# Moving row constants, root guess and statistics between VectorE, GpSimd and ScalarE in a graph-attention and mixture-of-experts kernel

## The reference

```
h   = layernorm(x) @ W.T + b_W
e   = leaky_relu((h @ a1)[:, None] + (h @ a2)[None, :] + b_a, slope 0.2)
x   = x + softmax(where(adj > 0, e, -9e15), axis=1) @ h
z   = layernorm(x)
p   = softmax(z @ gate_w + gate_b); keep the two largest of 16, scaled to sum 1
out = x + sum over the two experts k of p_k * ((silu(z @ w1_k) * (z @ w2_k)) @ w3_k)
```

## Time and profile before

| | |
|---|---|
| time of the kernel, median of 3 runs | 1756.96 us (1756.46 to 1762.68) |
| the profiled execution, own time | 1744.11 us |
| span of its profile | 1742.3 us |
| TensorE busy | 1519.6 us (87%) |
| VectorE busy | 1443.1 us (83%) |
| ScalarE busy | 1332.6 us (76%) |
| GpSimd busy | 464.9 us (27%) |

### The profile page before, as it was taken

The page is one execution under the profiler, slowest core; times in us unless marked ns, Lnnn a source line. Parts: engine busy times, 40 slices in busy tenths (PEclk is TensorE's granted clock), DMA queues, the critical chain, the costliest instruction groups (busy, mean ns, idle before and its releaser), DMA issues.

```text
span 1742.3 us, 24866 instructions
## 1 busy us (share of the span) xinstructions
PE 1519.6 (87%) x8110; PEld 840.4 (48%) x8111; DVE 1443.1 (83%) x1946; ACT 1332.6 (76%) x1804; POOL 464.9 (27%) x641
## 2 busy tenths in 40 slices
PE   5678699899989998998999899989999948999991
PEld 5545354455445444544454455445555525666660
DVE  6799999989998999999899989997896753444445
ACT  4989899889888997998799889878786634555550
POOL 6600000210024031403220240114024253555551
PEclk9998999999999999999999999999999978999995
DMA  6888778748865784887488648855432434222227
GB/s 187 299 311 302 238 255 265 234 141 259 262 204 181 255 266 135 260 245 253 133 272 271 207 156 268 255 180 147 135 113 75 139 68 159 74 73 74 74 73 298
DMA packets 127715, 339.40 MB, mean 195 GB/s; under 512 B 16962, under 2 KB 48898, under 8 KB 127490
## 3 DMA queue, kind: packets, MB, share of 16 engines
q1 hardware_dynamic: 106208, 304.06, 54.4%
q0 software_dynamic: 17056, 27.17, 5.9%
q10 hardware_dynamic: 4354, 6.92, 1.2%
HBM read 309.57 MB, written 28.51 MB: 194 GB/s over the span
## 4 chain that ended last, share of the span: by engine, by line
PE 39%; DVE 34%; issue 16%; POOL 4%; ACT 3%; DMA 3%; SPq 0%; ACTq 0%; DVEq 0%; POOLq 0%
PE pair L975 18%; DVE probs L1279 17%; DVE ring L1223 14%; PE pair L1054 8%; PE pair L960 5%; PE pair L1070 4%; ACT ring L713 2%; PE pair L1061 2%; DMA ring<-res_d 1%; PE pair L1050 1%; DVE part L1223 1%; POOL numT L601 1%; POOL numT L604 1%; POOL ln L591 1%; PE pair L987 1%
## 5 line engine op out<-in xcount | busy, mean ns | idle before, releaser
L975 PE MATMUL pair<-probs,X 128*128 128x512 f32 x2048 | 1009.5, 610 | 0.8 <-ACT probs L764 0.7
L764 ACT ACTIVATE probs<-probs,ebias 128x1024 f32<-128x1024 f32 (+1 forms) x576 | 601.2, 1046 | 179.5 <-DVE probs L1279 177.6
L1279 DVE SCALAR_TENSOR_TENSOR probs<-s1row,ns,pair 128x1024 f32<-128x1024 f32 (+1 forms) x576 | 654.5, 1154 | 68.2 <-PE pair L960 66.3
L1223 DVE CUSTOM_DVE_ANT_0 ring<-urow,ring 128x2048 int8<-128x2048 f16 x256 | 586.1, 2291 | 10.2 <-ACT ring L713 10.2
L713 ACT ACTIVATE ring<-stage,neghalf 128x1024 int8<-128x1024 int32 x512 | 575.2, 1141 | 1.5 <-DMA stage<-in_adj 1.2
L960 PEld LDWEIGHTS pair<-diag,ring 128*128 128x128 fp8e5 x4096 | 264.2, 98 | 461.6 <-DVE probs L1279 238.8
L975 PEld LDWEIGHTS pair<-probs,X 128*128 128x128 f32 x2048 | 345.9, 191 | 217.7 <-issue 215.6
L960 PE MATMUL pair<-diag,ring 128*128 128x128 bf16 x4096 | 325.9, 220 | 125.9 <-DVE probs L1279 103.0
L1553 DVE COPY probs<-pair 128x256 f32<-128x256 f32 x144 | 61.1, 425 | 138.6 <-PE pair L1061 126.2
L685 POOL DMA_INDIRECT res_d<-probs x144 | 138.9, 964 | 133.4 <-ACT probs L868 129.7
L1054 PE MATMUL pair<-ring,probs 128*128 x288 | 159.3, 635 | 4.9 <-issue 4.0
(11 more groups left out here) (237 smaller groups left out, 769.3 us busy)
## 6 DMA issues: line engine op xcount, KB each, us to landing
stage<-in_adj SPq DMA_DIRECT2D x512, 512.0 KB, 4.4
probs<-xd_d SPq DMA_DIRECT2D x144, 65.0 KB, 1.9
ring<-res_d SPq DMA_DIRECT2D x16, 512.0 KB, 9.5
ring<-in_L_ffn_w SPq DMA_DIRECT2D x2, 2048.0 KB, 11.7
ring<-xmid_d SPq DMA_DIRECT2D x1, 4096.0 KB, 13.5
out<-ring ACTq DMA_DIRECT2D x8, 512.0 KB, 6.8
s1row<-s_d SPq DMA_DIRECT2D x7, 512.0 KB, 7.2
xres<-in_x POOLq DMA_DIRECT2D x7, 512.0 KB, 12.1
```

The lines of the kernel that those rows point to most:

```text
L764: act.activation(probs[:, n % PR, 0:wide], probs[:, n % PR, 0:wide], ACT.Exp, bias=ebias[:, j:j + 1], scale=RISE).then_inc(probs_ready, 1)
L975: m = pe.matmul(acc[q][:, lo:hi], X[:, j, :], probs[:, n % PR, lo:hi], start=(j == 0), stop=(j == NT - 1))
L1223: dve.tensor_tensor_reduce(m, urow[:, c * CH:(c + 1) * CH], m, CODE, NO_EDGE, ALU.subtract, ALU.max, part[:, k, c:c + 1]).then_inc(piece_d ...
L1279: dve.scalar_tensor_tensor(out=probs[:, n % PR, 0:wide], in0=s1row[:, q, 0:wide], scalar=ns2[:, j:j + 1], in1=Tp[n % 2][:, 0:wide], op0=AL ...
```

## The change

- Row constants: VectorE keeps only the maximum over chunks (`row_max`, at step 58); the rest of `row_end` moves to GpSimd as six operations, with `kS` and `kB` of the other sign. It is called for block 0 and 1 before GpSimd's loop, and for block b+2 between the destinations and the scatter of block b.
- Root guess: `new_root` goes; GpSimd computes the guess in one operation.
- Gate base: `gate_base` goes, with the wait at VectorE's first `logits`. Each block's `gate_logits` multiplies by the standard deviation itself. `sd0` and `nm0` move to tiles of their own, as they now live to the end.
- Signs of block 0: one half per group for `g` = 0 to 4, two from `g` = 5 as before.
- Second layer norm: `new_stats` goes. ScalarE forms each row's sum (`row_sums`, two tiles a step from step 31 in place of VectorE's step 36) and, when GpSimd has given the negative mean, the sum of squared differences (`row_squares`, from step 36). Both write a throw-away result to PSUM and the sum through the accumulator output. `row_sums` waits for the same `xres_in` as `new_stats` did. In host 8 they stand at 26 and 31, and the later steps move by two.
- `last_norm` has two operations and one wait more.

```
-    CHAIN_AT = 59
+    CHAIN_AT = 58
+    DIAG_AT = 61
-            return dict(stats=36, per=2, root=42, top=46, ranks=54, slots=56, weights=61)
-        return dict(stats=26, per=2, root=32, top=38, ranks=46, slots=48, weights=51)
+            return dict(stats=31, per=2, squares=36, top=46, ranks=54, slots=56, weights=61)
+        return dict(stats=26, per=2, squares=31, top=40, ranks=48, slots=50, weights=53)
...
+            def row_end(b):
+                w = slice(0, BLOCKS[b])
+                pool.wait_ge(vmax, b + 1)
+                plink(pool.tensor_scalar(mrow[:, w], rmax[:, w], kS[:, 0:1], kB[:, 0:1], ALU.mult, ALU.add))
+                pool.tensor_scalar(crow[:, w], mrow[:, w], 1.0 / RISE - 1.0, None, ALU.mult)
+                plink(pool.tensor_tensor(hmax[:, w], scol[:, ROW0[b]:ROW0[b + 1], 0], mrow[:, w], ALU.subtract))
+                plink(pool.tensor_scalar(hmax[:, w], hmax[:, w], 0.0, None, ALU.max))
+                plink(pool.tensor_tensor(crow[:, w], crow[:, w], hmax[:, w], ALU.subtract))
+                if b >= 1:
+                    pool.wait_ge(d_ready, b)
+                pool.tensor_scalar(cdiag[:, w], crow[:, w], Cc[:, 0:1], EDGE_ONE, ALU.add, ALU.mult
+                                   ).then_inc(c_ready, 1)
...
+                pool.wait_ge(sum_rows, b + 1)
+                pool.tensor_scalar(r(2), st2[:, 0:n, 0], -1.0 / D, None, ALU.mult).then_inc(nm_ready, 1)
                 pool.wait_ge(st2_ready, b + 1)
...
+                plink(pool.tensor_scalar(r(3), st2[:, 0:n, 1], 1.0 / D, EPS, ALU.mult, ALU.add))
+                plink(pool.tensor_scalar(ln2I[:, 4, 0:n], ln2I[:, 3, 0:n], -0.5, GUESS, ALU.mult, ALU.add))
...
-                pool.tensor_tensor(lg, pgs[:, 0:n, :], cols[:, ROW0[b]:ROW0[b + 1], 2:2 + E], ALU.add)
-                plink(pool.tensor_tensor(t2, per_e(sg[:, :], b), per_t(ln2[:, 2, 0:n], b), ALU.mult))
+                rows = slice(ROW0[b], ROW0[b + 1])
+                pool.tensor_tensor(ln2[:, 0, 0:n], ln2[:, 2, 0:n], nm0[:, rows], ALU.subtract)
+                plink(pool.tensor_tensor(lg, cols[:, rows, 2:2 + E], per_t(sd0[:, rows], b), ALU.mult))
+                pool.tensor_tensor(t2, per_e(sg[:, :], b), per_t(ln2[:, 0, 0:n], b), ALU.mult)
+                plink(pool.tensor_tensor(lg, lg, pgs[:, 0:n, :], ALU.add))
...
-                if 5 <= g < NG:
-                    for i in range(early, early + 2):
+                if g < NG:
+                    for i in range(early, early + (2 if g >= 5 else 1)):
                         sign(0, i)
-                    early += 2
+                    early += 2 if g >= 5 else 1
...
+            def row_sums(b, k):
+                if k == 0:
+                    act.wait_ge(xres_in[b % 2], 16 * (b // 2 + 1))
+                    act.wait_ge(proj_read, ROUND0[b + 1])
+                ins = act.activation(acc[b % 2][:, k * P:(k + 1) * P], xres[:, b % 2, k, 0:D], ACT.Identity,
+                                     accum_out=st2[:, k, 0:1])
+                if k == BLOCKS[b] - 1:
+                    ins.then_inc(sum_rows, 1)
+
+            def row_squares(b, k):
+                if k == 0:
+                    act.wait_ge(nm_ready, b + 1)
+                ins = act.activation(acc[b % 2][:, k * P:(k + 1) * P], xres[:, b % 2, k, 0:D], ACT.Square,
+                                     bias=ln2[:, 2, k:k + 1], scale=1.0, accum_out=st2[:, k, 1:2])
+                if k == BLOCKS[b] - 1:
+                    ins.then_inc(st2_ready, 1)
```

More of the change, by code:

```diff
@@ L667, in scatter_last @@
                             in_=xres[:, LQ, c * LN + k, :], in_offset=None).then_inc(disp[c], 16)
-            gate_base()
+            row_end(0)
+            row_end(1)
             for b in range(LAST):
@@ L676, in _ @@
                 destinations(b, 0)
+                if b + 2 < NB:
+                    row_end(b + 2)
                 for c in range(2):
@@ L828, in _ @@
                     if b >= 1:
-                        k = j - route_units(b)["top"]
-                        if 0 <= k < BLOCKS[b - 1]:
-                            normal_rows(b - 1, k)
+                        units = route_units(b)
+                        for k in range(BLOCKS[b - 1]):
+                            if j == units["stats"] + k // units["per"]:
+                                row_sums(b - 1, k)
+                            if j == units["squares"] + k // units["per"]:
+                                row_squares(b - 1, k)
+                            if j == units["top"] + k:
+                                normal_rows(b - 1, k)
                     if b >= 1 and j == route_units(b)["slots"]:
                         weights(b - 1)
-                    if b + 1 < NB and j == CHAIN_AT + 2:
+                    if b + 1 < NB and j == DIAG_AT:
                         make_diag(b + 1)
@@ L1214, in _ @@
             wlink(dve.tensor_scalar(Cc[:, :], Cc[:, :], 1.0, None, ALU.add))
-            dve.tensor_scalar(kS[:, :], S2, -1.0 / (CODE * U_SPAN), None, ALU.mult)
-            wlink(dve.scalar_tensor_tensor(out=kB[:, :], in0=S2, scalar=-(1.0 - U_MID) / U_SPAN, in1=b2,
-                                           op0=ALU.mult, op1=ALU.add))
+            dve.tensor_scalar(kS[:, :], S2, 1.0 / (CODE * U_SPAN), None, ALU.mult)
+            wlink(dve.scalar_tensor_tensor(out=kB[:, :], in0=S2, scalar=(1.0 - U_MID) / U_SPAN, in1=b2,
+                                           op0=ALU.mult, op1=ALU.subtract))
             def maxima(b, i):
@@ L1224, in maxima, with row_max @@
                                          ALU.subtract, ALU.max, part[:, k, c:c + 1]).then_inc(piece_done, 1)
[L1226 to L1228 removed]
+            def row_max(b):
                 w = slice(0, BLOCKS[b])
[L1230 to L1236, removed]
[L1237 to L1252 removed]
+                dve.wait_ge(piece_done, PIECE0[b + 1])
+                if b >= 1:
+                    dve.wait_ge(c_ready, b)
+                dve.tensor_reduce(rmax[:, w], part[:, w, :], AX.X, ALU.max).then_inc(vmax, 1)
             ready = 0
@@ L1264, in _ @@
                 maxima(0, i)
-            for step in range(5):
-                row_end(0, step)
+            row_max(0)
             def logits(b, j):
@@ L1415, in route @@
             def route(b, j, units):
-                for k in range(BLOCKS[b]):
-                    if j == units["stats"] + k // units["per"]:
-                        new_stats(b, k)
-                if j == units["root"]:
-                    new_root(b)
                 for step in range(TOPS):
@@ L1439, in _ @@
                     if b + 1 < NB and j == CHAIN_AT:
-                        row_end(b + 1, 0)
-                        row_end(b + 1, 1)
-                    if b + 1 < NB and j == CHAIN_AT + 1:
-                        for step in range(2, 5):
-                            row_end(b + 1, step)
+                        row_max(b + 1)
                     if b >= 1:
@@ L1463, in last_norm @@
                 ins.then_inc(st2_ready, 1)
[L1464 removed]
+                rlink(dve.tensor_tensor(lg, cols[:, ROW0[LAST]:NT, 2:2 + E], per_t(sd0[:, ROW0[LAST]:NT], LAST),
+                                        ALU.mult))
+                last_rlink()
+                dve.tensor_tensor(lg, lg, pgs[:, 0:LN, :], ALU.add)
                 dve.wait_ge(st2_ready, LAST + 1)
```

76 lines of the change are left out of this document (14 added, 62 removed).

## The result

The changed kernel takes 1783.78 us (median of 4 runs, 1781.48 to 1787.24), the kernel before 1759.82 us (4 runs, 1756.46 to 1764.73) beside it: 1.0138 times the time, 95% interval 1.0112 to 1.0163. That is 24.0 us slower; forecast were 23, and 1780 us.

What follows compares the result with a forecast made beforehand. VectorE was taken to bound hosts 1 to 6 up to about step 57, TensorE hosts 7 and 8. Terms -4.9 - 1 + 22.5 + 6 + 0.4 = +23.0 us, added to the median of the runs, gave 1780 us, range 1752 to 1803.

Steps and rivals of the forecast that it cites:

- The stall: Step 31, hosts 2 to 6: ScalarE stands at row_sums for the DMA into xres; logits 44 late by 3.6 us.
- S: Time in host 2 when ScalarE goes on after the DMA lands: 459.9 us, bounds 458.0 and 463.2.
- VectorE's relief of 1.9 us: Statistics and root VectorE no longer computes, ahead of logits 44: 1.9 us a host, forecast as lost in the wait.
- The price of a sum: ScalarE's cost for each of 16 new sum and square operations: taken 0.40 us, bounds 0.25 and 0.57.
- Hosts 2 to 6: Stall plus 0.9 us for later gate logits: +4.5 us per host, +22.5 for five, bounds -0.7 and +10.6 each.
- Host 7: TensorE leads; ScalarE stands 5 to 6 us, plus two sums and an exponential (1.8): +6 us, 3 to 9.
- Host 1: Its DMA is issued some 35 us ahead of step 31: no stall, VectorE saves time, -1 us.
- Host 8 and the end: Host 8: no accumulating DMA and TensorE leads, 0; last_norm has two small operations on the path, +0.4 us.
- Prologue: Before host 0: early signs hidden, small operations cheaper, diagonals start at 88.9 against 93.76 us, -4.9 us.
- the slip of the loop: Prologue: maxima starve GpSimd, the 13th group gets its tiles at about 60.7 us, the loop slips by 2.4 us.
- the fast case: Rival at step 31, hosts 2 to 6: stall absorbed, VectorE's relief arrives; -16 us, 1741 us; chance 0.13.
- The slow case: Rival: DMA takes 12 to 14 us, sums cost 0.5 or more; +9 per host, +50, 1807 us; chance 0.12.

Runs made afterwards that it cites:

- x_sums: Changed kernel with sums and squares reading X in place of xres, without the DMA wait, so the second normalisation's statistics are wrong; 1741.04 us, ratio 0.9930.
- x_sums_again: Same kernel as x_sums, run once more for a profile in which the stages can be read; 1729.82 us in one execution.
- after_again: The changed kernel once more, no edit; 1770.87 us against 1744.65 for the kernel before beside it, ratio 1.0148.
- ahead: Changed kernel, sums in fours (steps 36, 37), squares at 39, 40, top at 48, gate base ahead of statistics, host 8 four tiles at once; 1721.88 us, ratio 0.9867.
- early_only: The kernel before with the five early signs alone, gate base and row constants left as they were; ratio 0.9972.
- c_before: The kernel before once more, no edit, for a second profile; 1755.99 us.
- the first set: Follow-up runs on one chip, among them c_before and x_sums; the kernel before took 1751.04 to 1762.33 us there.
- the later two sets: Follow-up runs on two other chips, among them x_sums_again, ahead, early_only and after_again; the kernel before took 1742.24 to 1750.48 and 1741.90 to 1753.07 us.

## Why the prediction was right, step by step

**Bound and place.** Right. The loss is in hosts 2 to 7, at the DMA into `xres`; `x_sums` removes it by taking away the wait alone.

**The stall.** Forecast: late by 3.6 us at logits 44 in host 2; measured 6.1. The path held, and three terms of its sum were off. The DMA landed 2.4 us later than taken (S at 451.14 + 11.15 = 462.29 on the scale of before, 459.9 forecast, inside the bound of 463.2): the median landing is shorter than before, 11.0 for 12.1, but in this host it took 12.9; that it is shorter because the loads dry up isn't shown, as it is 11.3 in `x_sums_again`, where nothing stands. The sixteen operations cost 16 x 0.34 = 5.4 instead of 6.4. From S to exponential 40 it is 23.1 us, which is 17 x 1.04 + 5.4 to the tenth. And from exponential 40 to logits 44 it is 4.4 instead of 3.4: its transposes were done at 477.85, but VectorE was at a maximum until 478.68.

That last term points at what the prediction had wrong here. It let VectorE's relief of 1.9 us be lost in the wait, because logits 44 would wait for what ScalarE's queue brings. But VectorE is at work again from logits 36 (457.60) on, with the longer share per step, and up to logits 45 (480.11) it is idle for 0.40 and 0.15 us only; in hosts 2 to 6 of `after_again` logits 45 starts 28.97 us after S within 0.01 each time and waits for TensorE for 0.17. The two queues meet there. With 1.8 us of statistics and root still in that stretch (22.4 us from logits 36 to 44 before, 21.1 now with 0.4 idle), logits 45 would have come 1.0 to 1.5 us later, an estimate from the idle time between logits 36 and 45, 0.3 to 0.8 us a host: more than half of the relief arrives.

The price of a sum had no row before. Now it has: 0.29 and 0.39 us from start to start (0.40 was taken for both). By the page "ScalarE: Activation LUTs" of the Trainium skill, section "What ACT_TABLE_LOAD costs", an operation takes 186 ns and 0.833 ns per element, 93 more per pointer operand, and overlaps by 93: 0.20 and 0.29 for the activations. One instruction of a single column to read the accumulator adds 186 less 93 ns, which gives, as an estimate, 0.29 and 0.385: the trace agrees from start to start. A free accumulator output, the case that the prediction worked out by that page of the Trainium skill, was wrong. So was its 465 ns for two pointer operands: the figures of the Trainium skill make 479, and the row has 479.

**Hosts 2 to 6.** Forecast +22.5, measured +24.1 (`after_again` against the first profile of before). That it comes so near is partly luck. The 0.9 us a host for later gate logits isn't paid in the changed kernel (0.34 us as before) and most of VectorE's relief does arrive, while the standing is longer than was taken: misses of both signs that nearly cancel.

**Host 7** +6 forecast, +5.9 measured. **Host 1** -1 and -1.7.

**Host 8 and the end.** Forecast +0.4, measured +2.5. This step failed in size: VectorE waits 2.7 us for the gate logits at step 40, which it didn't before, though the top was moved two steps back. I took TensorE's lead for cover and didn't follow GpSimd's chain there. By `ahead` the wait can be taken away, without a gain that reaches the end of the kernel; the rest of the 2.5 is open, and `early_only`, which leaves host 8 as it was, has 1.9 more there itself.

**Prologue.** Forecast -4.9, measured -6.7. The early signs are hidden (the `sign` of group 5 starts at 36.86 us, 36.85 before) and VectorE runs eight maxima in a row, as forecast; the two small operations take 0.22 and 0.28 us (0.6 forecast for both). What failed is the slip of the loop, 0.5 us and not 2.4. GpSimd is starved as forecast; its timeline, while the maxima run:

```profile
42.12 13.48 POOL L538 TENSOR_SCALAR X<-X,nm,probs 128x127 f32<-128x127 f32 x2
```

Two tiles take 13.5 us here, and the third is done at 60.2. But of the last 16 tiles three and not two were done by 42, so the 13th group had its four at 48.9 and not at 60.7, and only the 14th, with its tiles at 61.1, came close behind its turn (TensorE waited 2.09 us for it): a miscount by one tile.

**Rivals.** The first, with the fast case, needed a landing within 7.5 us; in the two profiles of the changed kernel none came under 8.1. The slow case needed both the full landing and a dear accumulator; it got the first in host 2 and not the second. The fast case is real all the same, five steps later: it needs another place for the sums, not a faster DMA.

**The level.** Adding the 23 us to the median and not to the first profile's 1744.1 is what made 1780 right; the profiles' own difference is 38.7, and 11.3 of it is level. Stage by stage the total is +27.4 against +23.0: the 3.2 of host 0, which nothing forecast and nothing explains, 2.1 behind host 7 and 1.6 in hosts 2 to 6 on one side, 1.8 in the prologue and 0.7 in host 1 on the other. That the medians beside each other give 24.0 is nearer than the steps deserve.

## What to carry to other kernels

An operation moved to an engine with time to spare brings its wait with it. On an in-order queue ask what the operation waits for and when that is there: VectorE did the same work in the kernel before five steps later and hardly met the DMA's 12 us: not once in the first profile, once for 0.6 us in `c_before`. Then follow the chain that starts at it: the best place here is one where the data have landed and the consumers are not yet due, and packing the work (fours for pairs) started that chain three steps earlier. Before stages of two profiles are compared, profile the old kernel twice, once beside the new one.

## What was not expected of the hardware

- A level of the runs: in the three usable profiles of the first set and in the changed kernel's first profile VectorE stands 2.7 to 3.8 us once a host from host 3 or 4 on (the trace puts it down to something remote, or to TensorE) and 4.0 to 4.9 us once in host 8 (remote); in none of the eight profiles of the later two sets, nor in the first profile of the kernel before. The level is worth some 10 us of 1750. What it is, and whether it belongs to a chip, stays open.
- TensorE's granted clock falls after the standing: behind 7.75 us of idle time the next four matmuls of a product take 3.78 us instead of 1.94, the clock of the host is 0.97 instead of 1.00, so part of it ran at 1.2 GHz and not at 2.4, and TensorE is busy for 151.0 us with work that takes 148.7 without the wait. Little of it can reach the host's time: in `after_again` logits 36 starts 5.97 to 6.46 us after the end of the standing (S), and logits 45 still 28.97 us after S each time.
- ScalarE's accumulator output costs one instruction of 186 ns, 0.09 us net.
